# Second layer's scan inputs: deltas from nine stacked bf16 partial products in one matmul, the sum in one pass on DVE, the product with u on POOL

## The chip, the cores and the metric

The kernel runs on one core of a Trainium2 chip. Its engines work at the same time, each on its own queue of instructions: PE (TensorE, matrix products), DVE (VectorE) and POOL (GpSimd) for element-wise passes, ACT (ScalarE) for functions and copies, and SP, which here only issues transfers. They wait for one another through semaphores. The metric is the time of one execution on the device, in microseconds (us).

## What is computed

The program is a chain of four layers over 32 images of 96 channels and 32 x 32 points. The change lies in layer 1, a selective scan over 1024 points in both directions. Its reference, cut to what matters:

```python
flat = xc.reshape(b, d, L)
flipped = xc[:, :, ::-1, ::-1].reshape(b, d, L)
xl = jnp.swapaxes(jnp.concatenate([flat, flat, flipped, flipped], axis=1), 1, 2)
x_dbl = xl @ W_x
dt_r = x_dbl[..., :dr]
Bm = x_dbl[..., dr:dr + n]
Cm = x_dbl[..., dr + n:]
delta = jax.nn.softplus(dt_r @ W_delta + b_delta)
y = _selective_scan(xl, delta, A, Bm, Cm, Dp)
```

`dr` is 6 and `n` is 16. For each image the stage in question makes `delta` (768 channels by 1024 points), the product `delta * u` (u is `xl`), and `Bm` and `Cm`, all for the scans that follow.

## The kernel before

The program is a row of stages; each loads from and stores to the chip's main memory. The stage here is `l1_scan_inputs` (its tiles carry the prefix `l1p_`). It has its order written out by hand, one function per engine. `turns` runs a function `turn(k, s)` for each image k, unrolled by four, from one image ahead to one behind. Inside it loops over T = 6 steps, one per tile of 128 channels: tiles 0 to 2 in forward order, 3 to 5 backward. `back(k, t, lag)` names the tile that lies `lag` steps behind step t (it may belong to the image before), so each engine handles tiles of different age in one step. `nth(q)` is the semaphore value that says that item q is done.

For one image the work is:

- PE, `project` (L1255), in step 1 for the next image: `px` (38 rows: 16 of B, 16 of C, 6 of dt) from u, with the weights of equal halves added up in `wsum`; eight f32 matmuls of 512 columns.
- ACT, `read` (L1309), at the end of step 2: copies `px` to `dts`. A row of ones beneath it carries the bias.
- PE, `deltas` (L1262), in step t for tile t+2: two f32 matmuls of 512 columns over the 7 rows of dt and ones, into one of two halves of `pd`.
- DVE: `dl` = max(`pd`, 0) (L1225), `ab` = -2 `dl` + `pd`, that is -|x| (L1228), both in the tile's own step. ACT: exp (L1323) and ln(1 + .) (L1325) of it into `ln`. POOL: `dl` = `dl` + `ln` (L1206), which is softplus.
- DVE: `du` = `dl` * u (L1234), three steps behind (DU = 3). PE: `turn_du` (L1271), eight transposes of it into `pt`, four behind (TURN = 4), ahead of the step's deltas in PE's queue. ACT: copy of `pt` to `dut` (L1317), five behind (OUT = 5), ahead of the step's exp.
- PE, `turn_b` (L1277), in step 3: eight small matmuls that transpose the rows of B; ACT copies the result (L1331). SP stores `dls`, `duts`, `crows` and `bts`, and loads u for three images ahead.

Which wait holds what: `deltas` waits until `ab` of the tile two before is made; `turn_du` waits for `du` and for the copy of the transposes before, since `pt` is single.

```python
pe.wait_ge(dtc, nth(m))
pe.wait_ge(absd, nth(T * m + v - 2))
```

Of the kernel before, what the change touches and what calls it, by code (L numbers as in the profile page):

```python
# [20 lines left out]
F8 = mybir.dt.float8e5  # L21
ALU = mybir.AluOpType
# [1088 lines left out]
def l1_scan_inputs(nc, u1, w, dls, duts, bts, crows, ident):  # L1111
# [3 lines left out]
    DT = slice(2 * N, XD + 1)  # L1115
    U_OF = (0, 0, 1)
    DU, TURN, OUT = 3, 4, 5

    with ExitStack() as stack:
        r = Room(nc, "l1p", stack)  # L1120
        u = r.sb("u", [128, UNROLL, 2, HW])
        dts = r.sb("dts", [XD + 1, 2, HW])
# [5 lines left out]
        wx = r.sb("wx", [128, T, XD]); wsum = r.sb("wsum", [128, 4, XD]); wd = r.sb("wd", [XD + 1, T, 128])  # L1128
# [8 lines left out]
        const, wsummed, xd, dtc, btm, btc, dtm, plus, absd, expd, lnd, sumd, dud, dutm, dutc, passed = r.step_sems(  # L1137
            "const", "wsummed", "xd", "dtc", "btm", "btc", "dtm", "plus", "absd", "expd", "lnd", "sumd", "dud", "dutm",
            "dutc", "passed")
        consts = [(wx[:, :, :], w["wx"]), (wd[DT, :, :], w["wd"]), (idt[:, :], ident)]  # L1140
# [7 lines left out]
        def in_order(s, t):  # L1148
            row = u[:, s % UNROLL, U_OF[t % HT], :]
            return row[:, ::-1] if t >= HT else row  # L1150

        with nc.Block() as block:
            @block.sync
            def _(sp):
# [6 lines left out]
                def turn(k, s):  # L1161
                    for t in range(T):
                        m, v = back(k, t, 3)
# [4 lines left out]
                        m, v = back(k, t, 6)  # L1168
                        if v % HT == HT - 1 and there(m):
                            g = v // HT  # L1170
                            sp.wait_ge(dutc, nth(T * m + v))
# [3 lines left out]
                        if t == 3 and there(k + 1):  # L1175
                            p = (s + 1) % 2
                            sp.wait_ge(dtc, nth(k + 1))
                            sp.sem_inc(passed, 1)
                            sp.dma_start(one(crows, k + 1), dts[N:2 * N, p, :]).then_inc(s_c[p], 16)
                            sp.wait_ge(dud, nth(T * (k - 1) + T - 1))  # L1180
                            sp.sem_inc(passed, 1)
                            if there(k + 3):
                                load(k + 3, s + 3)
# [17 lines left out]
            def _(pool):  # L1201
                def turn(k, s):
                    if there(k):
                        for t in range(T):
                            pool.wait_ge(lnd, nth(T * k + t))
                            pool.tensor_tensor(dl[:, t, :], dl[:, t, :], ln[:, t % 3, :], ALU.add).then_inc(sumd, 1)  # L1206
# [4 lines left out]
            def _(dve):  # L1211
                dve.memset(dts[DT, :, :], 1.0).then_inc(const, 1)
# [1419 lines left out]
```

## Time and profile before

| | us |
|---|---|
| median of three runs | 22473.82 |
| lowest and highest | 22467.68, 22474.48 |
| profiled execution | 22468.44 |
| its span, first to last instruction | 22466.7 |

The profile of one execution lists for each engine when it was at work, and what it waited for when it was not. The granted clock is a share of TensorE's full 2.4 GHz; its two levels are 0.50 (1.2 GHz) and 1.00. Over the whole span PE is busy 19369.5 us (86%), DVE 17043.7 (76%), ACT 16452.2 (73%) and POOL 13494.5 (60%), at a mean granted clock of 0.913. These are means over stages that differ much: the stage of the change takes some 1220 us of the 22467, and what the change is worth is read there. In the trace an f32 matmul appears as two records; a group's mean ns is that of one record.

### The profile page before, as it was taken

What the parts mean: (1) busy time and instruction counts of PE and PEld (TensorE: products, weight loads), DVE (VectorE), ACT (ScalarE), POOL (GpSimd) and SP (SyncE); (2) the same over time, 40 slices, a digit from 0 to 9 for tenths busy, and PEclk for the clock granted to TensorE, in tenths of its full rate; (3) what the DMA queues carried; (4) which work ended last, traced back from release to release, by engine and by line L of the source; (5) the groups of instructions that cost most, each with busy time, mean ns of one, the idle gap of its engine ahead of it and who ended that gap; (6) DMA issues with size and microseconds to landing.
All of it is one profiled execution on the core that took longest, in us unless ns stands there. A gap on an engine that the chain in (4) does not pass through costs nothing. (4 is left out here: it accounts for less than half of the span.)

```text
span 22466.7 us, 264583 instructions
## 1 busy us (share of the span) xinstructions
PE 19369.5 (86%) x73736; PEld 10093.5 (45%) x73736; DVE 17043.7 (76%) x13056; ACT 16452.2 (73%) x25994; POOL 13494.5 (60%) x5860
## 2 busy tenths in 40 slices
PE   7788887788886889989998988889899888889798
PEld 2344443344442334434445555555555555235353
DVE  2777777777775659937669999999999998446666
ACT  6488886688882455556569999999999998124545
POOL 0277774377771558806349999999999998000101
PEclk8699998799996899998679999999999999569899
DMA  4566665566666341174543333333333333520202
GB/s 123 187 206 191 204 193 177 191 204 194 203 198 175 91 162 77 62 260 186 198 178 121 121 121 121 121 120 115 118 122 121 120 122 111 134 76 28 84 29 79
DMA packets 842186, 3171.46 MB, mean 141 GB/s; under 512 B 101515, under 2 KB 124541, under 8 KB 815750
## 3 DMA queue, kind: packets, MB, share of 16 engines
q1 hardware_dynamic: 805510, 3029.73, 41.2%
q10 hardware_dynamic: 35328, 125.85, 1.7%
q8 instruction: 591, 9.68, 0.2%
q14 instruction: 757, 6.20, 0.1%
HBM read 2316.32 MB, written 838.88 MB: 140 GB/s over the span
## 5 line engine op out<-in xcount | busy, mean ns | idle before, releaser
L1525 DVE TENSOR_TENSOR_SCAN l1s_h<-l1s_da,l1s_pd 128x1024 f32<-128x1024 f32 x3072 | 6862.7, 2275 | 389.5 <-PE l1s_pd L1460 378.6
L1556 ACT ACTIVATE l1s_dm<-l1s_dut,l1s_bt 128x384 f32<-128x384 f32 x8192 | 4449.7, 605 | 16.6 <-DMA l1s_u<-u 11.3
L1460 PE MATMUL l1s_pd<-l1s_id,l1s_dm 128*128 128x128 f32 x24576 | 3197.1, 277 | 609.9 <-ACT l1s_dm L1556 358.3
L1460 PEld LDWEIGHTS l1s_pd<-l1s_id,l1s_dm 128*128 128x128 f32 x24576 | 2756.3, 142 | 2033.7 <-DVE l1s_h L1525 1061.2
L1546 ACT ACTIVATE l1s_da<-l1s_dl,l1s_a 128x1024 f32<-128x1024 f32 x3072 | 3504.0, 1141 | 18.4 <-DVE l1s_h L1525 17.1
L1436 POOL TENSOR_TENSOR l1s_sm<-l1s_h 128x1024 f32<-128x1024 f32 x1024 | 2429.0, 2372 | 264.6 <-DVE l1s_h L1525 253.9
L1441 POOL TENSOR_TENSOR l1s_pb<-l1s_h,l1s_cc 128x1024 f32<-128x1024 f32 x1024 | 2433.4, 2376 | 1.1
L1445 POOL TENSOR_TENSOR l1s_pa<-l1s_sm,l1s_cc 128x1024 f32<-128x1024 f32 x1024 | 2428.8, 2372 | 0.0
L2318 POOL TENSOR_TENSOR l0sb_pr<-l0sb_h,l0sb_cc 128x1024 f32<-128x1024 f32 x768 | 1812.2, 2360 | 775.7 <-DVE l0sb_h L2391 718.0
L2318 POOL TENSOR_TENSOR l0sf_pr<-l0sf_h,l0sf_cc 128x1024 f32<-128x1024 f32 x768 | 1812.1, 2360 | 774.9 <-DVE l0sf_h L2391 713.6
L849 POOL TENSOR_TENSOR dw_acc<-dw_acc,dw_prod 128x961 f32<-128x961 f32 (+3 forms) x704 | 1572.8, 2275 | 1092.6 <-ACT dw_prod L802 1085.0
L1470 PE MATMUL l1s_py<-l1s_pb,l1s_id 128*128 128x512 f32 x4096 | 1991.4, 609 | 166.4 <-POOL l1s_pb L1441 162.6
L2081 POOL CAST ffn_h<-ffn_z 128x1024 fp8e5<-128x1024 f16 x128 | 181.6, 1420 | 3241.9 <-DVE ffn_z L2101 3221.4
L1470 PE MATMUL l1s_py<-l1s_pa,l1s_id 128*128 128x512 f32 x4096 | 1927.3, 593 | 0.0
L780 PE MATMUL dw_pc<-dw_vol,dw_diag 128*128 128x512 f32 (+7 forms) x4224 | 1763.7, 580 | 57.8 <-DMA dw_vol<-n 30.6
L2444 ACT ACTIVATE l0sb_dm<-l0sb_dut,l0sb_bt 128x192 f32<-128x192 f32 x4096 | 1491.8, 441 | 317.3 <-PE l0sb_pd L2328 307.9
L2444 ACT ACTIVATE l0sf_dm<-l0sf_dut,l0sf_bt 128x192 f32<-128x192 f32 x4096 | 1491.8, 440 | 316.2 <-PE l0sf_pd L2328 306.8
L879 DVE SCALAR_TENSOR_TENSOR dw_pc<-dw_vol,dw_wt,dw_pc 128x961 f32<-128x961 f32 (+5 forms) x1280 | 1484.7, 1235 | 209.2 <-PE dw_pc L780 205.2
L2347 PE MATMUL l0sb_py<-l0sb_pr,l0sb_id 128*128 128x512 f32 x3072 | 1579.0, 596 | 0.0
L2347 PE MATMUL l0sf_py<-l0sf_pr,l0sf_id 128*128 128x512 f32 x3072 | 1578.0, 596 | 0.0
L2385 DVE TENSOR_TENSOR_SCAN l0sb_h<-l0sb_da,l0sb_st,l0sb_pd 128x512 f32<-128x512 f32 x768 | 982.0, 1279 | 617.1 <-ACT l0sb_da L2434 568.4
L2385 DVE TENSOR_TENSOR_SCAN l0sf_h<-l0sf_da,l0sf_st,l0sf_pd 128x512 f32<-128x512 f32 x768 | 982.0, 1279 | 616.0 <-ACT l0sf_da L2434 567.8
(291 smaller groups left out, 31044.3 us busy)
## 6 DMA issues: line engine op xcount, KB each, us to landing
l1s_cc<-crows SPq DMA_DIRECT2D x1024, 512.0 KB, 3.7
l0sf_cc<-l0crowsf SPq DMA_DIRECT2D x512, 512.0 KB, 5.0
l0sb_cc<-l0crowsb SPq DMA_DIRECT2D x512, 512.0 KB, 5.0
l0sf_cc<-l0crowsf SPq DMA_DIRECT2D x512, 256.0 KB, 6.4
l0sb_cc<-l0crowsb SPq DMA_DIRECT2D x512, 256.0 KB, 6.3
dls<-l1p_dl SPq DMA_DIRECT2D x192, 512.0 KB, 6.9
duts<-l1p_dut SPq DMA_DIRECT2D x64, 1536.0 KB, 7.0
l1s_dut<-duts SPq DMA_DIRECT2D x64, 1536.0 KB, 7.2
```

The lines of the kernel that those rows point to most:

```text
L1436: pool.tensor_tensor(sm[:, rnd % 2, :], h[:, rnd * HT % 4, :], h[:, (rnd * HT + 1) % 4, :], ALU.add)\
L1441: pool.tensor_tensor(pb[:, rnd % 2, :], h[:, (rnd * HT + 2) % 4, :], cc[:, rnd % 4, :], ALU.mult)\
L1445: pool.tensor_tensor(pa[:, rnd % 2, :], sm[:, rnd % 2, :], cc[:, rnd % 4, :], ALU.mult)\
L1460: mm = pe.transpose(pd[:, s % 2, blk * 128:blk * 128 + 128], dm[:, rnd % 2, blk, j * 128:j * 128 + 128], idt[:, :])
L1470: mm = pe.matmul(target[:, hs], idt[:, :], prods[:, rnd % 2, hs], start=(n == 0), stop=(n == N - 1))
L1525: dve.tensor_tensor_scan(h[:, s % 4, :], da[:, j, :], pd[:, s % 2, :], 0.0, ALU.mult, ALU.add)\
L1546: act.activation(da[:, j, :], dl[:, half, j, :], ACT.Exp, scale=a[:, HT * half + j, n:n + 1])\
L1556: ins = act.activation(dm[:, rnd % 2, blk, :], dut[:, half, blk, :], ACT.Identity, scale=bt[:, half, blk, n:n + 1])
L2318: pool.tensor_tensor(pr[:, s % 4, :], h[:, s % 6, :], cc[:, rnd % 4, j, :], ALU.mult).then_inc(prod, 1)
L2347: mm = pe.matmul(py[:, j, HALVES[half]], idt[:, :], pr[:, s % 4, HALVES[half]], start=(n == 0), stop=(n == N - 1))
L2385: dve.tensor_tensor_scan(h[:, s % 6, LO], da[:, s % 4, LO], pd[:, 0, :], st[:, rnd // N, rnd % N, j:j + 1], ALU.mult, ALU.add).then_inc(sc ...
L2444: ins = act.activation(dm[:, rnd % 2, blk, cols], dut[:, rnd // N, blk, cols], ACT.Identity, scale=bt[:, rnd // N, q, blk, rnd % N:rnd % N ...
```

## The change

`dt` is held as three bf16 parts that add up to it: high, middle and low. The weights of the projection now have 128 columns, so `px` has 128 rows: 32 of B and C, and three groups of 32 that each hold dt three times (18 rows) and three rows of ones. The ones come from an added matmul with one row (`one_at`, `one_row`) in each half of the projection. Rows 32 to 127 of `parts` become, group by group, the high part (ACT's copy, which rounds), the middle part (DVE: `rest` = `px` - high; ACT: its copy) and the low part (DVE: `rest` - middle). `wd` is split into three bf16 parts likewise, once, by DVE at the start of the stage. Each group meets all three parts of the weights, so one bf16 matmul over 128 rows adds nine partial products and the bias. B and C go to a tile of their own, `bc`, through a second copy on ACT.

-|x| is made by setting the sign bit of `pd` on DVE; max and sum are one DVE pass, in the next step; POOL multiplies by u. The copy of `pt` goes to DVE for even tiles and stays on ACT for odd ones, in both cases four steps behind (OUT = 4), behind the step's other work. `read` moves ahead of step 2's exp, as two copies.

The diff, cut to its core:

```diff
-    DU, TURN, OUT = 3, 4, 5
+    TURN, OUT = 4, 4
+    GROUPS = slice(64, 128)
+
+    SIGN = -2 ** 31
...
             def _(pool):
...
-                            pool.wait_ge(lnd, nth(T * k + t))
-                            pool.tensor_tensor(dl[:, t, :], dl[:, t, :], ln[:, t % 3, :], ALU.add).then_inc(sumd, 1)
+                            q = T * k + t
+                            pool.wait_ge(sumd, nth(q))
+                            pool.wait_ge(dutm, nth(q - 2))
+                            pool.tensor_tensor(du[:, t % 2, :], dl[:, t, :], in_order(s, t), ALU.mult).then_inc(dud, 1)
...
             def _(dve):
...
                         if there(k):
                             q = T * k + t
-                            dve.wait_ge(s_dl[t], k * 16)
-                            dve.wait_ge(dud, nth(q - T))
                             dve.wait_ge(dtm, nth(q))
-                            dve.tensor_scalar(dl[:, t, :], pd[:, t % 2, :], 0.0, None, ALU.max).then_inc(plus, 1)
-                            dve.wait_ge(plus, nth(q))
                             dve.wait_ge(expd, nth(q - 3))
-                            dve.scalar_tensor_tensor(out=ab[:, t % 3, :], in0=dl[:, t, :], scalar=-2.0,
-                                                     in1=pd[:, t % 2, :], op0=ALU.mult, op1=ALU.add).then_inc(absd, 1)
-                        m, v = back(k, t, DU)
+                            dve.tensor_scalar(ab[:, t % 3, :].bitcast(I32), pd[:, t % 2, :].bitcast(I32), SIGN, None, ALU.bitwise_or).then_inc(absd, 1)
+                        m, v = back(k, t, 1)
                         if there(m):
-                            dve.wait_ge(sumd, nth(T * m + v))
-                            dve.wait_ge(dutm, nth(T * m + v - 2))
-                            dve.tensor_tensor(du[:, v % 2, :], dl[:, v, :], in_order(s + (t - DU) // T, v), ALU.mult)\
-                               .then_inc(dud, 1)
+                            q = T * m + v
+                            dve.wait_ge(s_dl[v], m * 16)
+                            dve.wait_ge(dud, nth(q - T))
+                            dve.wait_ge(lnd, nth(q))
+                            dve.scalar_tensor_tensor(out=dl[:, v, :], in0=pd[:, v % 2, :], scalar=0.0, in1=ln[:, v % 3, :],
+                                                     op0=ALU.max, op1=ALU.add).then_inc(sumd, 1)
+                        m, v = back(k, t, OUT)
+                        if v % 2 == 0 and there(m):
+                            dve.wait_ge(dutm, nth(T * m + v))
+                            dve.wait_ge(s_du[v // HT], m * 16)
+                            dve.tensor_copy(*place(s, v)).then_inc(evened, 1)
+                        if t == 2 and there(k + 1):
+                            dve.wait_ge(hi, nth(k + 1))
+                            dve.wait_ge(mid, nth(k))
+                            dve.tensor_tensor(rest[GROUPS, :], px[GROUPS, :], parts[GROUPS, p, :], ALU.subtract).then_inc(res, 1)
+                        if t == 3 and there(k + 1):
+                            dve.wait_ge(mid, nth(k + 1))
+                            dve.tensor_tensor(parts[96:128, p, :], rest[96:128, :], parts[96:128, p, :], ALU.subtract)\
+                               .then_inc(lo, 1)
...
             def _(pe):
...
-                                mm = pe.matmul(px[0:XD, hs], wsum[:, c, :], row[:, hs], start=(c == 0), stop=(c == 3))
+                                pe.matmul(px[:, hs], wsum[:, c, :], row[:, hs], start=(c == 0), stop=False)
+                            mm = pe.matmul(px[:, hs], one_at[:, :], one_row[:, hs], start=False, stop=True)
...
-                        pe.wait_ge(dtc, nth(m))
-                        pe.wait_ge(absd, nth(T * m + v - 2))
+                        pe.wait_ge(lo, nth(m))
+                        pe.wait_ge(sumd, nth(T * m + v - 2))
                         for hs in HALVES:
-                            mm = pe.matmul(pd[:, v % 2, hs], wd[DT, v, :], dts[DT, (s + (t + 2) // T) % 2, hs],
+                            mm = pe.matmul(pd[:, v % 2, hs], wdel[:, v, :], parts[:, (s + (t + 2) // T) % 2, hs],
                                            start=True, stop=True)
...
             def _(act):
...
+                        if t == 2 and there(k + 1):
+                            act.wait_ge(xd, nth(k + 1))
+                            act.wait_ge(dtm, nth(T * (k - 1) + T - 1))
+                            act.activation(parts[:, p, :], px[:, :], ACT.Copy).then_inc(hi, 1)
+                            act.wait_ge(btm, nth(k - 1))
+                            act.wait_ge(s_c[p], (k + 1 - p) * 8)
+                            act.activation(bc[:, p, :], px[0:2 * N, :], ACT.Copy).then_inc(bcd, 1)
                         if there(k):
...
                         if t == 2 and there(k + 1):
-                            read()
+                            act.wait_ge(res, nth(k + 1))
+                            act.activation(parts[GROUPS, p, :], rest[GROUPS, :], ACT.Copy).then_inc(mid, 1)
+                        m, v = back(k, t, OUT)
+                        if v % 2 and there(m):
+                            act.wait_ge(dutm, nth(T * m + v))
+                            act.wait_ge(s_du[v // HT], m * 16)
+                            act.activation(*place(s, v), ACT.Copy).then_inc(odded, 1)
```

How the rows stand on two engines, in the middle of the stage. DVE before, a step and the first two passes of the next:

```order
L1225 TENSOR_SCALAR l1p_dl<-l1p_pd 128x1024
L1228 SCALAR_TENSOR_TENSOR l1p_ab<-l1p_dl,l1p_pd 128x1024
L1234 TENSOR_TENSOR l1p_du<-l1p_dl,l1p_u 128x1024
L1225 TENSOR_SCALAR l1p_dl<-l1p_pd 128x1024
L1228 SCALAR_TENSOR_TENSOR l1p_ab<-l1p_dl,l1p_pd 128x1024
```

Each step is the same three passes, max, -|x| and the product with u; none reads `pt`. DVE in the change, from step 1 to step 4 of an image (L1258 is abs, L1265 the sum of the tile before, L1271 the copy of transposes, L1275 `rest`, L1278 `lo`):

```order
L1258 TENSOR_SCALAR l1p_ab<-l1p_pd 128x1024
L1265 SCALAR_TENSOR_TENSOR l1p_dl<-l1p_pd,l1p_ln 128x1024
L1258 TENSOR_SCALAR l1p_ab<-l1p_pd 128x1024
L1265 SCALAR_TENSOR_TENSOR l1p_dl<-l1p_pd,l1p_ln 128x1024
L1271 COPY l1p_dut<-l1p_pt 128x8x128
L1275 TENSOR_TENSOR l1p_rest<-l1p_px,l1p_parts 64x1024
L1258 TENSOR_SCALAR l1p_ab<-l1p_pd 128x1024
L1265 SCALAR_TENSOR_TENSOR l1p_dl<-l1p_pd,l1p_ln 128x1024
L1278 TENSOR_TENSOR l1p_parts<-l1p_rest,l1p_parts 32x1024
L1258 TENSOR_SCALAR l1p_ab<-l1p_pd 128x1024
L1265 SCALAR_TENSOR_TENSOR l1p_dl<-l1p_pd,l1p_ln 128x1024
L1271 COPY l1p_dut<-l1p_pt 128x8x128
```

The product with u has gone, and in every second step a copy that reads PE's transposes stands between the sum and the next abs.

PE in the change around the projection, from step 1 to step 4 (L1316 is `turn_du`, L1307 `deltas`, L1299 and L1300 the projection, L1323 `turn_b`):

```order
L1316 MATMUL l1p_pt<-l1p_id,l1p_du 128x128 x8
L1307 MATMUL l1p_pd<-l1p_parts,l1p_wdel 128x512 x2
L1299 MATMUL l1p_px<-l1p_u,l1p_wsum 128x512 x4
L1300 MATMUL l1p_px<-l1p_one,l1p_oneat 128x512
L1299 MATMUL l1p_px<-l1p_u,l1p_wsum 128x512 x4
L1300 MATMUL l1p_px<-l1p_one,l1p_oneat 128x512
L1316 MATMUL l1p_pt<-l1p_id,l1p_du 128x128 x8
L1307 MATMUL l1p_pd<-l1p_parts,l1p_wdel 128x512 x2
L1316 MATMUL l1p_pt<-l1p_id,l1p_du 128x128 x8
L1307 MATMUL l1p_pd<-l1p_parts,l1p_wdel 128x512 x2
L1323 MATMUL l1p_px<-l1p_id,l1p_bc 128x16 x8
L1316 MATMUL l1p_pt<-l1p_id,l1p_du 128x128 x8
```

The order on PE is as before, but for the two added matmuls of the projection. What changed for it is which semaphore the deltas wait for.

## Rows read from the trace of the kernel before

**Rows 1.** Stretches: us, busy us of each engine (count), mean granted clock, DMA share, GB/s
```profile
10500.00:11500.00 1000.00, 998.66 (x2772) 466.29 (x2770) 604.57 (x477) 511.67 (x529) 372.85 (x159) 0.64 0.52 196
...
12500.00:13000.00 500.00, 449.38 (x2231) 277.56 (x2229) 475.31 (x218) 499.44 (x767) 487.32 (x210) 1.00 0.34 125
```

**Rows 2.** Groups by line, 10500 to 11500: engine, shapes, count, busy us, mean ns, idle before
```profile
L1262 PE MATMUL l1p_pd<-l1p_dts,l1p_wd 7*128 7x512 f32 x636 | 511.8, 946 | 0.2 <-DVE l1p_ab L1228 0.2
L1206 POOL TENSOR_TENSOR l1p_dl<-l1p_dl,l1p_ln 128x1024 f32<-128x1024 f32 x159 | 374.3, 2354 | 630.4 <-ACT l1p_ln L1325 630.4
L1271 PE MATMUL l1p_pt<-l1p_id,l1p_du 128*128 128x128 f32 x1272 | 263.2, 375 | 1.2 <-ACT l1p_dut L1317 1.1
...
L1228 DVE SCALAR_TENSOR_TENSOR l1p_ab<-l1p_dl,l1p_pd 128x1024 f32<-128x1024 f32 x159 | 194.1, 1221 | 11.8
L1323 ACT ACTIVATE l1p_ln<-l1p_ab 128x1024 f32<-128x1024 f32 x159 | 167.1, 1051 | 34.7 <-DVE l1p_ab L1228 25.4 <-POOL l1p_dl L1206 9.2
...
L1317 ACT ACTIVATE l1p_dut<-l1p_pt 128x1024 f32<-128x1024 f32 x159 | 161.9, 1018 | 183.3 <-PE l1p_pt L1271 182.8
```

**Rows 3.** Waits, 10500 to 11500: who for whom, total us, times, longest
```profile
ACT l1p_dts L1309 <- PE l1p_px L1255: 266.2, 27, 10.7
DVE l1p_du L1234 <- PE l1p_pt L1271: 208.5, 27, 8.6
```

**Rows 4.** Timeline, one step: start us, duration, engine, line, operation, shapes, idle before
```profile
10985.56 1.97 PE L1271 MATMUL l1p_pt<-l1p_id,l1p_du 128*128 128x128 f32 x8
10985.66 1.22 DVE L1225 TENSOR_SCALAR l1p_dl<-l1p_pd 128x1024 f32<-128x1024 f32 x1 [1.55 <-PE l1p_pd L1262]
10987.01 1.22 DVE L1228 SCALAR_TENSOR_TENSOR l1p_ab<-l1p_dl,l1p_pd 128x1024 f32<-128x1024 f32 x1
...
10987.45 3.78 PE L1262 MATMUL l1p_pd<-l1p_dts,l1p_wd 7*128 7x512 f32 x4
...
10991.16 1.97 PE L1271 MATMUL l1p_pt<-l1p_id,l1p_du 128*128 128x128 f32 x8
```

**Rows 5.** Timeline, the projection of an image and what follows it
```profile
10996.77 9.28 PE L1255 MATMUL l1p_px<-l1p_u,l1p_wsum 128*38 128x512 f32 x16
...
11005.98 1.10 PE L1271 MATMUL l1p_pt<-l1p_id,l1p_du 128*128 128x128 f32 x8
...
11007.00 1.98 PE L1262 MATMUL l1p_pd<-l1p_dts,l1p_wd 7*128 7x512 f32 x4
...
11007.18 1.22 DVE L1234 TENSOR_TENSOR l1p_du<-l1p_dl,l1p_u 128x1024 f32<-128x1024 f32 x1 [7.83 <-PE l1p_pt L1271]
```

**Rows 6.** Timeline, DVE's and POOL's passes one image apart
```profile
10972.58 2.36 POOL L1206 TENSOR_TENSOR l1p_dl<-l1p_dl,l1p_ln 128x1024 f32<-128x1024 f32 x1 [11.72 <-ACT l1p_ln L1325]
...
10973.75 2.27 DVE L1234 TENSOR_TENSOR l1p_du<-l1p_dl,l1p_u 128x1024 f32<-128x1024 f32 x1
...
11011.42 2.27 DVE L1234 TENSOR_TENSOR l1p_du<-l1p_dl,l1p_u 128x1024 f32<-128x1024 f32 x1
```

**Rows 7.** Stretches of 1.5 us: the clock column before and in a projection
```profile
10972.00:10973.50 1.50, 1.50 (x18) 1.33 (x16) 1.47 (x2) 1.41 (x2) 0.92 (x1) 1.00 0.78 235
...
10975.00:10976.50 1.50, 1.50 (x8) 1.17 (x7) 1.50 (x2) 1.25 (x3) 0.41 (x1) 0.50 0.92 336
...
11000.50:11002.00 1.50, 1.50 (x3) 0.31 (x2) 0.00 (x0) 0.00 (x0) 0.00 (x0) 0.74 0.00 0
```

**Rows 8.** Timeline, 512-column fp8 matmuls of the last stages, low level and high
```profile
20952.20 0.59 PE L2145 MATMUL ffn_ph<-ffn_x,ffn_w 96*128 96x512 fp8e5 x2
...
20958.29 1.91 PE L2145 MATMUL ffn_ph<-ffn_x,ffn_w 96*128 96x512 fp8e5 x4
```

**Rows 9.** Timeline, weight loads of 16-row matmuls, high level here and low in layer 0
```profile
10420.22 1.52 PEld L1277 LDWEIGHTS l1p_px<-l1p_id,l1p_dts 16*128 16x128 f32 x13 [2.14 <-ACT l1p_dts L1309]
...
1023.77 2.56 PEld L442 LDWEIGHTS l0pf_pt<-l0pf_id,l0pf_dts 16*128 16x128 f32 x13 [0.84 <-issue]
```

**Rows 10.** Timeline, the stage's first projection
```profile
10409.77 9.21 PE L1255 MATMUL l1p_px<-l1p_u,l1p_wsum 128*38 128x512 f32 x16 [22.43 <-DMA l1p_u<-u]
```

More of the change, by code:

```diff
@@ L1121, in l1_scan_inputs @@
         u = r.sb("u", [128, UNROLL, 2, HW])
-        dts = r.sb("dts", [XD + 1, 2, HW])
+        parts = r.sb("parts", [128, 2, HW], BF16); rest = r.sb("rest", [128, HW]); bc = r.sb("bc", [2 * N, 2, HW])
         ab, ln = (r.sb(n, [128, 3, HW]) for n in ("ab", "ln"))
@@ L1136, in l1_scan_inputs @@
         s_du = [r.dma_sem(f"du{g}") for g in range(2)]
[L1137 to L1140, printed above, removed]
+        const, wready, xd, hi, bcd, res, mid, lo, btm, btc, dtm, absd, expd, lnd, sumd, dud, dutm, evened, odded, passed = r.step_sems(
+            "const", "wready", "xd", "hi", "bcd", "res", "mid", "lo", "btm", "btc", "dtm", "absd", "expd", "lnd", "sumd", "dud",
+            "dutm", "evened", "odded", "passed")
+        consts = [(wx[:, :, :], w["wx"]), (wd[:, :, :], w["wd"]), (which[:, :], w["which"]), (idt[:, :], ident)]
         ready = 16 * len(consts)
@@ L1162, in turn @@
                     for t in range(T):
-                        m, v = back(k, t, 3)
+                        m, v = back(k, t, 2)
                         if there(m):
@@ L2502, in build @@
     dls1 = dram("dls1", (IMAGES, 6, 128, HW)); ys1 = dram("ys1", (IMAGES, 4, 128, HW))
-    ws = {n: w[f"{n}_1"] for n in ("wx", "wd", "alog", "skip", "ln_g", "ln_b", "wo")} | {"avg192": w["avg192"]}
+    ws = {n: w[f"{n}_1"] for n in ("wx", "wd", "which", "alog", "skip", "ln_g", "ln_b", "wo")} | {"avg192": w["avg192"]}
     l1_scan_inputs(nc, u1, ws, dls1, duts, bts, crows, w["ident"])
@@ L2588, in arranged @@
     w["l1dw_b"] = twice(v["L1_conv_b_dw"])
-    w["wx_1"] = tiles(bc_first(v["L1_conv_W_x"])[order], 6)
-    w["wd_1"] = cat([v["L1_conv_W_delta"], v["L1_conv_b_delta"][None]])[:, order].reshape(RANK + 1, 6, 128)
+    wx, wd = v["L1_conv_W_x"], np.zeros((128, 4 * DI), f)
+    thrice = [np.tile(wx[:, :RANK], 3), np.zeros((4 * DI, 32 - 3 * RANK), f)]
+    w["wx_1"] = tiles(cat([wx[:, RANK:], *thrice * 3], 1)[order], 6)
+    which = np.zeros((128, 3), f)
+    for j in range(3):
+        for group in range(3):
+            rows = slice(32 + 32 * group + RANK * j, 32 + 32 * group + RANK * (j + 1))
+            wd[rows], which[rows, j] = v["L1_conv_W_delta"], 1
+        wd[32 + 3 * RANK + j], which[32 + 3 * RANK + j, j] = v["L1_conv_b_delta"], 1
+    w["wd_1"], w["which_1"] = wd[:, order].reshape(128, 6, 128), which
     w["alog_1"] = tiles(v["L1_conv_A_log"][order], 6)
```

79 lines of the change are left out of this document (46 added, 33 removed).

## The prediction

> **What bounds it now.** The change touches one stage, `l1_scan_inputs`, whose trace runs from 10404 to about 11625 us. I read it in four steps.
>
> First the stretch view [rows 1]. In 1000 us of this stage PE is busy 998.66 us, DVE 604.57, ACT 511.67 and POOL 372.85, at a mean granted clock of 0.64. PE is the bound, and it runs mostly at the lower of its two levels. The scan stage at 12500 us stands beside it at 1.00.
>
> Second, the period of one image. Two like passes of `du` start at 10973.75 and 11011.42 us [rows 6], so an image takes 37.67 us; 32 of them are 1205 us, the whole stage but its ends.
>
> Third, what fills a period. In an ordinary step at the low level, the eight transposes start at 10985.56, the delta matmuls (four records for two f32 matmuls) at 10987.45 and take 3.78 us, and the next transposes start at 10991.16 [rows 4]: 5.60 us a step, all of it PE. DVE's passes take 1.22 us each and ACT's 1.05 or 1.02 [rows 2]; they wait for PE and have room. Once per image comes the projection, 9.28 us [rows 5].
>
> Fourth, who waits across that projection. DVE's `du` waits 7.83 us for the transposes behind it [rows 5], 208.5 us in total, and ACT's copy of its result 266.2 us [rows 3]. So while PE projects, the others already stand still; only PE's own work is saved by a faster matmul.
>
> The clock: 0.50 at 10975, while PE is never idle, 0.74 in the 1.5 us from 11000.50, some 4.5 us into the projection, and 1.00 at 10972, behind the projection of the image before [rows 7].
>
> **PE's saving.** Deltas go from f32 with 7 rows to one low-precision pass with 128 rows. The nearest rows are the fp8 matmuls of 512 columns: four in 1.91 us at the low level, two in 0.59 at the high one [rows 8]. With 0.63 us for the last one, the four are 0.43 apart, so two take 1.06 us to be ready, and occupy PE for 0.86, instead of 3.78 and 3.7. That is 2.85 us a step, 17 us an image if all steps were cold. Two things go back. The two added one-row matmuls cost 0.43 or 0.21 us each, 0.5 together. And `turn_b` now reads partitions 0 to 15 beside deltas that fill all rows; before it ran interleaved with the 7-row deltas. Alone, 13 of its weight loads take 1.52 us at the high level and 2.56 at the low one [rows 9], so its 16 cost 2.0 or 3.2 us. If PE remained the bound, an image would need at the low level 6 x (1.97 + 0.86) + 3.2 + 9.8 = 30 us. It won't, and that is the core of this prediction.
>
> **The new chain.** Before, deltas(t+2) waited for `absd`(t), made in DVE's step t. Now they wait for `sumd`(t), and DVE makes that one step later, after abs(t+1); and abs(t+1) needs deltas(t+1). So PE and DVE take turns: deltas, abs, sum, deltas. Second, DVE now copies the transposes of even tiles, in its queue directly behind the sum. Those transposes stand in PE's queue behind the deltas that this very sum releases. DVE therefore waits for deltas plus transposes, copies, and only then does the next abs, which holds the exp, ln, sum and deltas behind it. I take 0.1 us for a hand-over to PE, 1.2 for each DVE pass (1.22 in [rows 2, 4]; the copy, the 64-row and the 32-row pass have no row of their own and are taken by their 1024 columns), and walk one image from the start of its projection, at the clock levels that the rows show there:
>
> (a) projection 9.3 + 0.5 = 9.8. (b) Transposes of tile 4 of the image before, which stand behind it: 1.0 (1.10 less overlap, [rows 5]). ACT's copy to `parts` and `bc`, then exp and ln of tile 2, run beside (b) and (c) and end 4.1 us after the projection, in time. (c) DVE: copy, `rest`, abs(3), sum(2): 4.8. (d) deltas(4) 0.1 + 1.06 = 1.2, beside DVE's `lo` pass of 1.2, then abs and sum 2.4: 3.6. (e) deltas(5) 0.96, `turn_b` 3.2, transposes 1.97, then copy, abs, sum 3.6: 9.7. (f) a step without a DVE copy: 1.2 + 2.4 = 3.6. (g) a step with one: 0.96 + 1.97 + 1.2 + 2.4 = 6.5. (h) as (f), 3.6. (i) deltas(3), in front of the next projection: 1.0.
>
> Sum 43.6 us against 37.67: +5.93 an image, +190 us for 32. In it are 9.0 us, at (e) and (g), in which DVE only waits for PE's deltas, `turn_b` and transposes; before, DVE's passes ran beside such work.
>
> **The rest.** POOL does the multiply by u instead of an add, 2.35 us a tile [rows 2]; half are read backwards, for which POOL has no row, but it is idle 63% of the stage and the transposes come three steps later, so even a doubled time is covered. ACT gives away three of six copies (3 x 1.02) and gets one more 1024-column copy of `px` and one of `rest`: about 19 us of 43.6, covered. On SP the stores of `dls` and `duts` move one step forward, behind waits that are by then met; a tile is stored a whole image before it is rewritten; nobody waits. The load of u three images ahead has slack. Once per run come seven weight passes of 768 columns, by 1.22 us for 1024 some 0.95 us each, four small ones and 128-column weights to load. The first projection waited for u anyway until 10409.77 [rows 10], which hides part; I take 5 us, bounds 0 and 10.
>
> Total: 190 + 5 = +195 us. The profiled execution took 22468.44 us, 1.7 outside its span, and lies 0.02% below the median 22473.82. On the median: 22669 us, 0.87% slower.
>
> **Rivals.** *The clock stays high* (B). The walk takes the low level from some microseconds behind the projection on. For the high level speaks the scan stage, where transposes and f32 matmuls of full height share PE at 1.00 [rows 1]; the new deltas are of full height too. Against it: PE would be at work for 20 of the 34 us between projections, 12 of them transposes, and it sat at 0.50 even while never idle [rows 4, 7]. All high, the terms become 7.5, 1.0, 4.8, 3.6, 7.2, 3.1, 5.2, 3.1 and 0.5, together 36.0 us: 1.67 less than now, or -53 + 5 = -48 us, 22426. Partly high ends between, up to 22600. Beside this stands the Trainium skill, TensorE: Matmul & The Clock Gate, Part 4: a transpose does not count as PE being busy for the clock. By that rule PE would look nearly idle between projections, and B would fall away for A's 22669; by the scan stage alone, B's 22426 would be the likelier. No row here shows a stretch of transposes alone.
>
> *DVE's 32-row pass collides with POOL* (C). It reads two SBUF tensors, and it is queued just where sum(2) releases POOL's multiply. The row for that: POOL works from 10972.58 to 10974.94, a DVE pass over two SBUF tensors started at 10973.75 and took 2.27 instead of 1.22, ending 1.08 after POOL [rows 6]. If POOL gets in first, `lo` ends 2.36 + 1.08 + 0.1 = 3.5 us after the sum instead of 1.2: +2.1 an image beyond the deltas, +67 us, 22736. It needs no semaphore that is late, so I expect DVE to be first. The Trainium skill says the same of the mechanism (GPSIMD Engine Reference, Specifications: the SBUF interfaces are shared, with contention for DVE instructions with two SBUF inputs), and the trace agrees with its 2.27 us.
>
> *The chain is hidden* (D). If the queues slip against each other so that DVE's passes run beside PE's work as now, the stage falls to the busiest engine: DVE 12 x 1.2 + 3 x 1.2 + 2.4 = 20.4 us, plus the projection, in which DVE waits, and hand-overs: about 31 us. (31 - 37.67) x 32 + 5 = -208 us, 22266. For it: all busy sums fall well under the period. Against: the waits in the order of the queues leave no slip; the copy of tile t-4 cannot start before sum(t-1) is done.
>
> *The matmul does not get shorter* would leave +190 as a lower bound, and I give it nothing apart.
>
> **How the numbers follow.** Forecast A, a period of 41.5 to 46 us, 22602 to 22746: 0.60. B 0.13: 0.05 faster, 0.06 within 0.2%, 0.02 slower. C 0.12. D 0.10. Something dearer still, such as a projection that rises to the high level later: 0.05. A, C, the parts of B that are not faster and half of the dear end make 0.83: 22450 to 22790. About 0.2%, 45 us, is what a measurement can tell from no change. Faster by more: 0.15 (D and B's part); within: 0.06; slower: 0.79. In the period's terms, slower needs more than 38.9 us.
>
> **What would show it.** In the changed trace: the delta matmuls near 1.1 us for two at the low level; PE busy about 70% of the stage, with idle time ended by DVE's sum; DVE's copy with about 3 us of idle ahead of it, 6 where `turn_b` stands in front, 10 across the projection; the clock near 0.6; a period near 43.6. A period under 38 at a clock of 0.9 is B; `lo` at over 2 us is C; a copy that waits for nothing is D, and the walk is wrong.

## The result, and the profile after

| | us |
|---|---|
| changed kernel, median of four runs | 22685.79 |
| lowest and highest | 22676.91, 22688.67 |
| kernel before, on the same chip, median of four | 22470.75 |
| ratio, with 95% interval | 1.0096 (1.0078 to 1.0113) |

It is 215 us slower, 0.96%; the forecast was 195 us slower, 22669 us. The span of the profiled execution grew from 22466.7 to 22684.9, by 218. From the first transfer of `l1_scan_inputs` to the first of the next stage it took 1234.0 us before (10402.90 to 11636.93) and takes 1451.8 now (10402.53 to 11854.28), 218 more as well. The scan stage at 12500 us has its 450 us of PE in 500 as before. So all of the loss lies in the stage that was changed.

The stretch view of the changed kernel (columns as in [rows 1]):

```profile
10500.00:11500.00 1000.00, 647.64 (x2090) 401.76 (x2124) 458.94 (x386) 421.71 (x430) 319.78 (x136) 0.61 0.43 169
12500.00:13000.00 500.00, 450.15 (x2223) 279.84 (x2222) 472.81 (x217) 497.59 (x764) 484.67 (x210) 0.99 0.33 116
```

Set against [rows 1]: PE has fallen from 998.66 to 647.64 us of 1000, at nearly the same clock, DVE from 604.57 to 458.94, ACT and POOL too. Every engine is less busy, and POOL's 136 passes in place of 159 say how much less gets done. No engine is near its bound any more; a chain of waits has taken its place.

The groups by line and the waits, 10500 to 11500, answer [rows 2] and [rows 3]:

```profile
L1316 PE MATMUL l1p_pt<-l1p_id,l1p_du 128*128 128x128 f32 x1088 | 243.5, 399 | 0.0
...
L1307 PE MATMUL l1p_pd<-l1p_parts,l1p_wdel 128*128 128x512 bf16 x238 | 126.7, 621 | 353.5 <-DVE l1p_dl L1265 353.5
...
L1271 DVE COPY l1p_dut<-l1p_pt 128x1024 f32<-128x1024 f32 x68 | 83.3, 1225 | 482.1 <-PE l1p_pt L1316 482.1
```

```profile
DVE l1p_dut L1271 <- PE l1p_pt L1316: 482.1, 68, 12.1
PE l1p_pd L1307 <- DVE l1p_dl L1265: 353.5, 136, 5.6
...
ACT l1p_parts L1352 <- PE l1p_px L1300: 236.8, 22, 10.8
```

The delta matmuls were 511.8 us of PE and are 126.7. Ahead of them PE idles 353.5 us, and all of it is ended by DVE's sum (L1265). DVE in turn stands 482.1 us ahead of its copy, for PE's transposes. PE and DVE take turns, as the forecast said. ACT's wait for the projection is no loss: it stood 266.2 us there before [rows 3].

One image on PE, from one projection to the next (start, duration; in brackets the idle time before and who ended it; of the pair of deltas at 11002.74 the first record is missing):

```profile
10972.26 5.89 PE L1299 MATMUL l1p_px<-l1p_u,l1p_wsum 128*128 128x512 f32 x8
10978.09 0.39 PE L1300 MATMUL l1p_px<-l1p_one,l1p_oneat 1*128 1x512 bf16 x1
10978.41 3.70 PE L1299 MATMUL l1p_px<-l1p_u,l1p_wsum 128*128 128x512 f32 x8
10982.04 0.38 PE L1300 MATMUL l1p_px<-l1p_one,l1p_oneat 1*128 1x512 bf16 x1
10982.36 1.09 PE L1316 MATMUL l1p_pt<-l1p_id,l1p_du 128*128 128x128 f32 x8
10988.54 1.03 PE L1307 MATMUL l1p_pd<-l1p_parts,l1p_wdel 128*128 128x512 bf16 x2 [5.09 <-DVE l1p_dl L1265]
10989.36 1.91 PE L1316 MATMUL l1p_pt<-l1p_id,l1p_du 128*128 128x128 f32 x8
10992.30 1.04 PE L1307 MATMUL l1p_pd<-l1p_parts,l1p_wdel 128*128 128x512 bf16 x2 [1.02 <-DVE l1p_dl L1265]
10993.27 3.59 PE L1323 MATMUL l1p_px<-l1p_id,l1p_bc 16*128 16x16 f32 x16
10996.79 1.97 PE L1316 MATMUL l1p_pt<-l1p_id,l1p_du 128*128 128x128 f32 x8
11002.74 0.63 PE L1307 MATMUL l1p_pd<-l1p_parts,l1p_wdel 128*128 128x512 bf16 x1 [3.98 <-DVE l1p_dl L1265]
...
11016.63 5.90 PE L1299 MATMUL l1p_px<-l1p_u,l1p_wsum 128*128 128x512 f32 x8
```

The same on DVE:

```profile
10983.49 1.22 DVE L1271 COPY l1p_dut<-l1p_pt 128x1024 f32<-128x1024 f32 x1 [12.11 <-PE l1p_pt L1316]
...
10988.51 1.22 DVE L1278 TENSOR_TENSOR l1p_parts<-l1p_rest,l1p_parts 32x1024 bf16<-32x1024 f32 x1
...
10998.80 1.22 DVE L1271 COPY l1p_dut<-l1p_pt 128x1024 f32<-128x1024 f32 x1 [6.55 <-PE l1p_pt L1316]
...
11003.50 1.22 DVE L1258 TENSOR_SCALAR l1p_ab<-l1p_pd 128x1024 int32<-128x1024 int32 x1 [1.22 <-PE l1p_pd L1307]
...
11008.69 1.23 DVE L1271 COPY l1p_dut<-l1p_pt 128x1024 f32<-128x1024 f32 x1 [2.84 <-PE l1p_pt L1316]
...
11027.86 1.22 DVE L1271 COPY l1p_dut<-l1p_pt 128x1024 f32<-128x1024 f32 x1 [12.11 <-PE l1p_pt L1316]
```

From copy to copy it is 44.37 us, where [rows 6] gave 37.67; by the count of tiles (136 / 6 images in 1000 us) the mean is 44.1. The copy waits 2.84, 6.55 and 12.11 us at the three places that the forecast named with 3, 6 and 10. Where no copy stands in between, it is abs that waits for the deltas, 1.22 us at 11003.50.

### The profile page after: what moved, and what is told of

It reads as the page before. It is cut to its first block and busy times, and to the rows that moved or that the text cites. A ratio compares the mean times of both kernels' runs of the same rounds, so it can differ in the third digit from the quotient of the medians.

```text
span 22684.9 us, 264136 instructions
## 1 busy us (share of the span) xinstructions
PE 19086.2 (84%) x73368; PEld 10096.3 (45%) x73416; DVE 16964.6 (75%) x13033; ACT 16430.4 (72%) x25962; POOL 13495.5 (59%) x5860
```

## The experiments

The change has two parts that can be had singly: the matmul (deltas from stacked bf16 parts, instead of f32 over 7 rows) and the order (which pass of DVE, ACT and POOL stands where, and what the deltas wait for). The forecast says that the order costs and the matmul saves. The first five runs below test the chain of waits. `deltas_twice` was meant to test it too, against two other accounts; its time did not follow the chain at a fixed clock, and the runs after it test the clock.

### The matmul alone: `only_stacked_deltas`

The kernel before, its order kept (max, -|x| and the product with u on DVE; copies on ACT five steps behind; deltas wait for `absd`), with `parts`, `rest`, `bc`, `wdel` and the bf16 matmul of the change:

```diff
-                            mm = pe.matmul(pd[:, v % 2, hs], wd[DT, v, :], dts[DT, (s + (t + 2) // T) % 2, hs],
+                            mm = pe.matmul(pd[:, v % 2, hs], wdel[:, v, :], parts[:, (s + (t + 2) // T) % 2, hs],
```

> The kernel before with the stacked bf16 deltas alone: projection to 128 rows, parts, rest, lo, bc and the one bf16 matmul per half, all as in the change; but the order of before for the rest: max and -|x| in two DVE passes in the tile's own step, the add on POOL, the product with u on DVE three steps behind, all copies of transposes on ACT five behind, deltas waiting for -|x|. rest stands in DVE's step 3 and lo in step 4. Chain theory: deltas no longer wait for the sum, PE runs two tiles ahead and its 17 us saving per image is kept: about 31.5 to 33 us an image, the program about 22280 to 22330 us, the fastest so far. Added-work theory: it carries all the added work (rest, lo, two copies, one-row matmuls, turn_b alone), so it would lose against the kernel before, above 22500. Clock theory: PE is as little busy as in the changed kernel or less, so its level stays low; if that were the loss it would show here too.

Measured: 22259.43 us, ratio 0.9908 (0.9891 to 0.9925). The matmul alone wins 211 us. The stretch view:

```profile
10500.00:11300.00 800.00, 621.21 (x2447) 365.00 (x2447) 699.17 (x523) 555.61 (x575) 375.09 (x157) 0.78 0.65 244
```

PE is busy 78% and DVE 87%: now DVE is close to the bound, with the three passes that it had before, `rest` and `lo`. The time lies 21 us below the range that was expected of the chain. The clock went to 0.78, though PE was busy less than before; the clock theory of the expectation had it stay low. So 22685.79 - 22259.43 = 426 us is what the order costs on top of this matmul.

### The order alone: `f32_deltas_new_order`

The changed kernel with `dts`, `wd` and the f32 matmuls over 7 rows of before (`rest` and `lo` fall away):

```diff
-                            mm = pe.matmul(pd[:, v % 2, hs], wdel[:, v, :], parts[:, (s + (t + 2) // T) % 2, hs],
+                            mm = pe.matmul(pd[:, v % 2, hs], wd[DT, v, :], dts[DT, (s + (t + 2) // T) % 2, hs],
```

> The kernel before with the new order alone: deltas stay two f32 matmuls over 7 rows, projection and dts as before (no parts, rest, lo, bc, no one-row matmuls), but -|x| by the sign bit, the sum on DVE one step later, the product with u on POOL, DVE copying even tiles and ACT odd ones four steps behind, ACT's read of the projection ahead of step 2's exp, deltas waiting for the sum. It is the fourth corner of a square: kernel before (f32, old order) 22471, only_stacked_deltas (bf16, old order) 22259, changed kernel (bf16, new order) 22686. Chain theory: the new order puts each 3.8 us of deltas on the chain; by the walk an image takes 55 us, the program about 23030 us. Additive theory (the order costs 22686 - 22259 = 427 us whatever the matmul is): about 22900 us. Added-work theory: the order adds no work, so about 22471.

Measured: 22994.7 us, ratio 1.0232 (1.0215 to 1.0249), 524 us slower than before. That lies between the 22900 of a fixed price for the order and the 23030 of the chain, nearer to the chain. DVE's timeline:

```profile
10974.66 1.23 DVE L1238 TENSOR_SCALAR l1p_ab<-l1p_pd 128x1024 int32<-128x1024 int32 x1 [3.96 <-PE l1p_pd L1278]
10975.80 1.21 DVE L1245 SCALAR_TENSOR_TENSOR l1p_dl<-l1p_pd,l1p_ln 128x1024 f32<-128x1024 f32 x1
10990.51 1.23 DVE L1251 COPY l1p_dut<-l1p_pt 128x1024 f32<-128x1024 f32 x1 [13.50 <-PE l1p_pt L1287]
```

DVE's pass on `pd` now waits 3.96 us: the whole of the deltas stands on the chain, as it should if PE and DVE take turns. In the order of before the f32 deltas overlap DVE's passes: its pass on `pd` waits 1.55 us [rows 4].

### The copies one step later: `copies_step_later`

```diff
-    TURN, OUT = 4, 4
+    TURN, OUT = 4, 5
```

> The changed kernel with OUT = 5 instead of 4: both copies of the transposes, DVE's and ACT's, stand one step later in their queues; nothing else differs. Chain theory: DVE's copy then reads transposes that PE made a step before, so the 2 to 3 us wait in front of it in every second step goes, and the one across the projection too; what stays is turn_b in front of the transposes of tile 0. By the same walk as in the prediction an image takes about 39.3 us instead of 44.3, the program about 22530 us (165 less than the changed kernel, 57 more than the kernel before). Clock theory (the loss comes from PE standing at its low level): the work and the level stay, so the time stays within 20 us of the changed kernel's 22686. Added-work theory (two ACT copies, rest, lo, the added one-row matmuls and turn_b alone are the loss): also no change, 22686.

Measured: 22530.54 us, ratio 1.0029 (1.0017 to 1.0041), what was expected almost to the microsecond, and 155 us less than the changed kernel. That it costs to have the copies where the change puts them is thereby shown (this run moves DVE's and ACT's together). But the size came out by luck, as PE's timeline shows:

```profile
10998.85 3.70 PE L1299 MATMUL l1p_px<-l1p_u,l1p_wsum 128*128 128x512 f32 x8
11002.49 0.38 PE L1300 MATMUL l1p_px<-l1p_one,l1p_oneat 1*128 1x512 bf16 x1
11009.13 1.94 PE L1316 MATMUL l1p_pt<-l1p_id,l1p_du 128*128 128x128 f32 x8 [6.26 <-ACT l1p_dut L1370]
```

A new wait has come: `pt` is single, and its copy for the odd tile 3, on ACT, has slipped behind ACT's two copies of `px`, exp and ln. PE waits 6.26 us for it once per image. On DVE `lo` takes 2.22 us beside POOL's multiply, where it took 1.22 in the changed kernel:

```profile
10972.67 2.22 DVE L1278 TENSOR_TENSOR l1p_parts<-l1p_rest,l1p_parts 32x1024 bf16<-32x1024 f32 x1
```

Against these two losses the clock rose, from 0.61 to 0.77 over the stage. The walk had neither the losses nor the rise.

### The same with `turn_b` early: `copies_later_turnb_early`

`OUT` = 5, and `turn_b` in step 2, between transposes and deltas, where PE waits anyway:

```diff
                             turn_du(m, v)
+                        if t == 2 and there(k + 1):
+                            turn_b()
                         m, v = back(k, t, -2)
...
-                        if t == 3 and there(k + 1):
-                            turn_b()
```

> As copies_step_later, and turn_b moved on PE from the end of step 3 to step 2, between the transposes of tile 4 and the deltas of tile 4, where PE waits about 5 us for DVE's sum behind the projection. Chain theory: its 3.6 us leave the chain, an image takes about 35.8 us, the program about 22416 us, faster than the kernel before (22471). Clock theory and added-work theory: PE's work is the same, no difference from copies_step_later.

Measured: 22493.46 us (ten runs), ratio 1.0009 (0.9999 to 1.0018): 77 us slower than expected. The expectation rested on the walk of the run before, which had no wait of PE for ACT's copy. The waits view shows that wait here too:

```profile
PE l1p_pt L1316 <- ACT l1p_dut L1370: 230.3, 78, 6.3
```

### The wait taken away: `copies_split_turnb_early`

DVE's copies five steps behind, ACT's four as in the change, `turn_b` early as above:

```diff
-    TURN, OUT = 4, 4
+    TURN, OUT, ODD = 4, 5, 4
...
-                        m, v = back(k, t, OUT)
+                        m, v = back(k, t, ODD)
                         if v % 2 and there(m):
```

> As copies_later_turnb_early, but only DVE's copies of the even tiles stand one step later (OUT = 5); ACT's copies of the odd tiles stay where the change has them (four steps behind). In copies_later_turnb_early PE waited 6.26 us behind each projection for ACT's copy of tile 3, which had moved behind ACT's reading of the projection; the run before it missed its 35.8 us an image for that reason. Chain theory: this wait goes, an image takes 34 to 36 us, the program 22360 to 22430 us, around 22391. If something else held it back: no gain over 22493.

Measured: 22357.81 us, ratio 0.9947 (0.993 to 0.9963), 2 us below the expected range. With DVE's copy out of the chain, ACT's copy left where it was and `turn_b` in PE's idle time, this order takes 328 us less than that of the change, though the deltas wait for the same sum. In its waits view the line PE <- ACT is gone and PE's wait for the sum is down from 353.5 us to 206.6, none longer than 2.3:

```profile
PE l1p_pd L1307 <- DVE l1p_dl L1265: 206.6, 178, 2.3
```

No run moves DVE's copy alone, so how the 328 us divide between it and `turn_b` is open. So are the 98 us that this run still takes more than `only_stacked_deltas`: the wait for the sum that is left is one candidate, but no run gives the deltas back their earlier release within this order.

### More work on PE: `deltas_twice` and `only_stacked_twice`

Each pair of delta matmuls is issued twice, with the same result, in the changed kernel and in `only_stacked_deltas`:

```diff
-                        for hs in HALVES:
+                        for hs in HALVES * 2:
```

> The changed kernel with each pair of delta matmuls issued twice, into the same place: 0.86 us more of PE at the low level per step, the result is the same. Chain theory: every one of the six pairs of an image lies on the chain, so +5.1 us an image, +165 us, about 22850. Idle theory (PE is busy 65% of this stage and has room): no change, 22686. Clock theory: full-height matmuls double their share; if that lifts PE's level between the projections, the time rises by much less than 165 us or falls, and the mean granted clock of the stage goes well above 0.61.

> only_stacked_deltas with each pair of delta matmuls issued twice, into the same place, the result is the same. In that kernel the stage's clock was 0.76 and PE waited for ACT's copies. Clock theory: the clock rises, transposes and turn_b get shorter and pay for the added matmuls: 22230 to 22260 us, the same or up to 0.1% faster than only_stacked_deltas. If the clock does not rise: 6 x 0.86 us of PE more an image, partly in its idle time, up to 22330 us.

Measured: `deltas_twice` 22688.5 us, ratio 1.0099 (1.0082 to 1.0116), the same as the changed kernel, where the chain at a fixed clock gave +165 us and the clock theory much less. `only_stacked_twice` took 22234.27 us, ratio 0.9894 (0.9878 to 0.9911): with 12 more matmuls an image it is no slower than `only_stacked_deltas`; the intervals of the two ratios overlap. The stretch views, first of `deltas_twice`, then of `only_stacked_twice`:

```profile
10500.00:11500.00 1000.00, 662.74 (x2378) 388.51 (x2379) 456.22 (x383) 420.59 (x429) 316.11 (x135) 0.71 0.43 169
```

```profile
10500.00:11300.00 800.00, 637.12 (x2797) 367.19 (x2850) 720.24 (x537) 572.40 (x592) 387.47 (x162) 0.90 0.67 250
```

The clock went from 0.61 to 0.71 and from 0.78 to 0.90. PE's timeline of `deltas_twice` shows where the added work was paid back:

```profile
10975.21 1.88 PE L1307 MATMUL l1p_pd<-l1p_parts,l1p_wdel 128*128 128x512 bf16 x4 [3.58 <-DVE l1p_dl L1265]
...
10979.63 1.04 PE L1307 MATMUL l1p_pd<-l1p_parts,l1p_wdel 128*128 128x512 bf16 x4 [0.83 <-DVE l1p_dl L1265]
10980.50 3.60 PE L1299 MATMUL l1p_px<-l1p_u,l1p_wsum 128*128 128x512 f32 x8
```

Four matmuls take 1.88 us at the low level, 0.85 more than two; but the first half of the projection takes 3.60 us, not 5.89, since the high level is there before it starts. In some images more was paid back: `turn_b` took 1.96 us at 10956.21 and 3.59 at 11000.76. From projection to projection it is 44.5 us on average (10533.58 to 11468.67, 21 images) and from 43.1 to 47.3 in single ones. So here added matmuls of full height raised the granted clock, while the kernel before stood at 0.64 with PE almost never idle [rows 1]. What differs is that its deltas used 7 rows of the array; the next runs test that.

### The rows of the f32 deltas: `f32_deltas_128_rows` and `f32_deltas_64_rows`

The kernel before, with the same f32 matmuls in the same order, over 128 or 64 rows instead of 7. The added rows hold B, C or ones, and their weights are zero. `turn_b` can no longer run beside the deltas in either. With 128 rows (with 64 the slice ends at 64, and the tiles and weights grow to match):

```diff
-    DT = slice(2 * N, XD + 1)
+    DT = slice(0, 128)
```

> The kernel before with its f32 delta matmuls over 128 rows instead of 7: dts and wd have 128 rows, the weights of all but the seven rows are zero, so the sums are the same; everything else as before. It asks what holds PE's clock at the low level between projections in the kernel before, where PE is never idle. Height theory (matmuls over few rows do not lift the clock; doubled full-height matmuls in deltas_twice lifted the stage's mean from 0.61 to 0.71): the clock goes to 0.9 or more, PE's work per image falls to about 27 us, DVE becomes the bound at 28 to 31 us, the program 22170 to 22270 us. Transpose theory (transposes alone hold it low, rows do not matter): the clock stays at 0.64, and turn_b no longer runs beside the deltas, 2 to 3 us more an image: 22540 to 22570 us.

> As f32_deltas_128_rows (22147.6 us, stage clock 0.99), but over 64 rows instead of 128: half the array's height. turn_b reads rows 0 to 15 and so still cannot run beside the deltas, exactly as with 128 rows. If the loss of that overlap, or anything but the height, lifted the clock, this run is at 22148 +- 25 us with a clock of 0.99. If the height decides, and by degrees, the clock lies between 0.64 and 0.99 and the time between 22200 and 22500 us (22471 before, plus up to 1.6 us an image for turn_b alone at the low level = 22520). My guess is the middle, 22330.

Measured: 128 rows 22147.6 us, ratio 0.9855 (0.9839 to 0.9872), the fastest of all and 22 us below the range that was expected; 64 rows 22488.87 us (ten runs), ratio 1.0008 (0.9998 to 1.0017), no change. Stretch view and two groups with 128 rows, then the stretch with 64:

```profile
10500.00:11300.00 800.00, 735.49 (x3028) 374.85 (x3027) 715.58 (x529) 569.08 (x587) 418.38 (x177) 0.99 0.72 273
```

```profile
L1234 DVE TENSOR_TENSOR l1p_du<-l1p_dl,l1p_u 128x1024 f32<-128x1024 f32 x178 | 312.1, 1754 | 59.3 <-PE l1p_pt L1271 59.3
...
L1271 PE MATMUL l1p_pt<-l1p_id,l1p_du 128*128 128x128 f32 x1417 | 190.8, 278 | 56.4 <-ACT l1p_dut L1317 56.4
```

```profile
10500.00:11300.00 800.00, 800.00 (x2179) 363.13 (x2177) 471.68 (x377) 404.81 (x418) 294.74 (x126) 0.68 0.52 194
```

With 64 rows PE is never idle and sits at 0.68, as before at 0.64 [rows 1]; with 128 rows it is at 0.99. The matmuls, their columns and their order are alike, so what decides here is the rows of the array that the deltas use. The loss of the overlap with `turn_b` is in both and doesn't do it. The 64-row result, 22489 us, lies at the dear end of its range, far from the 22330 that was guessed: 64 rows lifted the clock hardly at all, and no height between 64 and 128 was run.

### Both: `f32_deltas_128_new_order`

`f32_deltas_new_order` with the deltas over 128 rows.

> The order of the change with f32 deltas over 128 rows (the weights of all rows but the 7 real ones are zero, the rows themselves hold B, C or ones); nothing else differs from f32_deltas_new_order (22994.7 us, stage clock 0.59), and the matmul instructions, their columns and their order are the same. Height theory (matmuls over 7 of 128 rows leave the clock low, full-height ones lift it): the stage rises to 0.9 or more, and the walk at the high level with two f32 matmuls at 1.96 us gives projection 7.2, transposes 1.0, DVE 3.6, then 4.5, 8.5, 4.5, 6.6, 4.5 and 2.0, together 42.4 us an image instead of the 53.9 that f32_deltas_new_order would need by its time: 22995 - 32 x 11.5 = 22627 us, 22590 to 22720 with a partly low stage. Rival (the rows don't matter, the clock of f32_deltas_128_rows rose only because turn_b no longer ran beside the deltas, or by its denser queue): here PE waits in turns anyway, so the clock stays near 0.6 and the time at 22995 us, with turn_b behind the deltas up to 23060.

Measured: 22763.97 us, ratio 1.013 (1.0114 to 1.0147). The clock rose from 0.59 to 0.82 and the time fell by 231 us, on a kernel whose PE waits in turns. The height of the deltas works here too. The time was 137 us above the 22627 of the walk and 44 above the range. The level doesn't hold through the whole image:

```profile
10977.34 1.95 PE L1293 MATMUL l1p_px<-l1p_id,l1p_dts 16*128 16x16 f32 x16
10979.23 1.09 PE L1287 MATMUL l1p_pt<-l1p_id,l1p_du 128*128 128x128 f32 x8
10983.90 3.78 PE L1278 MATMUL l1p_pd<-l1p_dts,l1p_wd 128*128 128x512 f32 x4 [3.58 <-DVE l1p_dl L1245]
...
10990.22 1.98 PE L1278 MATMUL l1p_pd<-l1p_dts,l1p_wd 128*128 128x512 f32 x4 [0.83 <-DVE l1p_dl L1245]
```

After `turn_b`, one set of transposes and 3.58 us of waiting, the deltas run at the low level, in 3.78 us; the pair after them is back at the high one, in 1.98.

The times side by side, in us:

| deltas | order of before | order of the change |
|---|---|---|
| f32, 7 rows | 22471 | 22995 |
| f32, 64 rows | 22489 | not run |
| f32, 128 rows | 22148 | 22764 |
| bf16 parts, 128 rows | 22259 | 22686 |

In each line that has both, the order costs: 524, 616 and 426 us. The price depends on the matmul that it is paid with; it isn't a fixed sum.

## Why the prediction was right, point by point

**What bounded it.** Right as far as it went: PE was never idle and the others waited. But "only PE's own work is saved by a faster matmul" left out that PE's work at 0.64 was long because of the clock, and the clock low because of the 7 rows. The fastest kernel here saves no PE instruction at all. PE was busy 65% of the changed stage, where the forecast named about 70%.

**The chain.** Right, and shown by three runs that touch it: `f32_deltas_new_order` put the longer deltas on it (DVE waits 3.96 us for them), `copies_step_later` and `copies_split_turnb_early` took the copy out of it. The copy's wait across the projection, 12.11 us, was named with 10; the walk's own terms (i), (a) and (b) add up to 11.8, so that was a slip in naming the wait and not in the sum.

**The terms.** From the two timelines of the changed kernel, measured against forecast: (a) projection 10.2 against 9.8; (b) 1.1 against 1.0; (c) 5.0 against 4.8; (d) 3.8 against 3.6; (e) 10.0 against 9.7, taking the deltas at 11002.74 to start 0.4 us earlier for the missing record; (f) 3.6 against 3.6; (g) 6.3 against 6.5; (h) 3.6 against 3.6; (i) 0.8 against 1.0. Together 44.4 us against 43.6. The two that were mis-sized most: the projection, 0.4 us over the 9.28 of [rows 5] plus 0.5 for the one-row matmuls, and `turn_b`, which took 3.59 us where the row scaled to 16 gave 3.2. By the mean of 44.1 the loss is 32 x (44.1 - 37.67) = 206 us. The walk held the clock at the levels of the rows of before, and the sum came out because the change stood at much the same level, 0.61 against 0.64; the experiments show that it can't be relied on.

**The deltas.** Two took 1.03 us at the low level; the estimate from fp8 rows [rows 8] was 1.06.

**The start.** First deltas at 10421.58 us before and at 10431.90 after: 10.3 us, where 5 was taken, with an upper bound of 10. The projection starts 4.9 us later, at 10414.63, since it waits for DVE's passes over the weights, though these took less than was assumed (0.41 to 1.04 us each). It takes 1.6 us longer. From its end to the first deltas 6.4 us pass instead of 2.6: `rest`, ACT's copy of it and a `turn_b` of 3.56 us (1.4 before) stand in front of them, which the term left out. 206 + 10 makes 216, beside the 215 measured.

**POOL, ACT, SP.** Hidden, as forecast. POOL's product with reversed reads took 2.35 us like the others, so the doubled time that was allowed for did not come.

**Rival B, the clock stays high.** It did not in the change: 0.61. The evidence named for B, that the new deltas are of full height, was the right thought. The evidence against it, "it sat at 0.50 even while never idle", was read wrongly: that low level was one of 7-row matmuls, and says nothing of matmuls over 128 rows. What kept B away was how little such work there is between the waits: one more pair of matmuls a step brought 0.71, and f32 pairs of full height in the same order brought 0.82. So A's time came out right with the clock held fixed, but B was set aside by a wrong argument, and where the work changed, a fixed clock failed: the +165 us that it gave for `deltas_twice` came out at nothing.

Of the rule that was weighed there, `f32_deltas_128_rows` is the run that bears on it. It spends 190.8 of 735.5 us of PE in transposes, 26%, the same share as before (263.2 of 998.66, [rows 1, 2]), and stands at 0.99. Transposes at this share are thus compatible with the high level, and by themselves don't explain why the kernel before stood low. The Trainium skill (TensorE: Matmul & The Clock Gate, Part 4) says that the full clock doesn't engage for transposes, which don't count as PE being busy in the same way. These runs don't contradict it, as other matmuls ran in every stretch above. Transposes alone stand only at the end of the stage, as in `f32_deltas_128_rows` behind its last deltas at 11285.50:

```profile
11288.59 1.06 PE L1271 MATMUL l1p_pt<-l1p_id,l1p_du 128*128 128x128 f32 x8 [1.13 <-ACT l1p_dut L1317]
11292.12 1.94 PE L1271 MATMUL l1p_pt<-l1p_id,l1p_du 128*128 128x128 f32 x8 [2.46 <-ACT l1p_dut L1317]
```

The level falls from 1.00 to 0.50 between these two sets and stays there for the four that follow. That fits the Trainium skill, but PE also waits 1.1 to 2.6 us ahead of each set, so it doesn't tell transposes from waits.

Part 1 of the same page of the Trainium skill describes a clock that follows how busy PE has been. By the trace that is not enough, if busy is taken as the profile shows it: with 7 rows PE was at work 998.66 us of 1000 at 0.64 [rows 1], and with 128 rows 735.49 of 800 at 0.99.

**Rival C.** In the changed kernel `lo` took 1.22 us: no collision, as expected, but not because DVE came first. The prediction had sum(2) release POOL's multiply. All 136 multiplies in the 1000 us waited for PE's transposes instead, since `du` has two buffers (681.4 us in total); around `lo`, at 10988.51, POOL was idle from 10985.88 to 10991.36. The mechanism is real: in `copies_step_later`, where the queues stand otherwise, `lo` took 2.22 us beside a multiply that started 1.21 us before it, and ended 1.08 us after that, as in [rows 6]. C's price was summed a little short: 3.5 less 1.2 is 2.3 us an image and not 2.1, so 22743 us.

**Rival D, the chain is hidden.** In the change no; but with the order of before around the new matmul it is what happened: 22259 us, where D gave 22266. That the two are so close is luck. D's sum for DVE was right for the change: 20.4 us an image against 20.2 measured (458.94 us in 22.7 images). `only_stacked_deltas` has other passes on DVE, busy 26.7 us an image (699.17 us, 523 passes of 20 an image), and DVE waits only 3.3 of the 9.8 us that D added for the projection (85.8 us, 26 times).

## What to carry to other kernels

When an engine gets faster, ask first who waits for whom in the new order: here the order took away 426 us and the faster matmul gave 211. Part of that was a copy put directly behind the pass that releases another engine's next work, so that the two engines took turns instead of working side by side. Let such a copy lag one step more, but check both engines that share the single buffer. And before saving work on PE in a stage whose granted clock is low while PE is never idle, look at how many rows its matmuls use: zero weights over the unused rows up to 128 are an edit of a few lines and gave 1.45%; up to 64 they gave nothing.

## What the runs showed of the hardware that I had not expected

- In this stage the granted clock went with the rows of the array that the deltas use, and not only with whether PE was at work. Same instructions, same order: 0.64 with 7 rows, 0.68 with 64 and 0.99 with 128. At a given level the rows didn't change the time: an f32 pair took 3.78 us at the low level with 7 rows [rows 4] and with 128, and 1.98 at the high level with 7 [rows 5] and with 128.
- More full-height work on PE cost nothing here: with the deltas issued twice the changed kernel took 22688.5 against 22685.8 us. The projection fell from 10.2 to 7.8 us in the image shown, and in some images `turn_b` from 3.59 to 1.96.
- `turn_b`, eight small matmuls in 16 records, ran interleaved with the 7-row deltas: before, the two together took 2.2 us at the high level (11009.93 to 11012.13), where a pair of deltas alone takes 1.98. Behind deltas that use its rows it takes 3.59 us at the low level, and 1.95 at the high one in `f32_deltas_128_new_order`. The Trainium skill (TensorE: Matmul & The Clock Gate, Part 3) describes small matmuls that run at the same time on different row groups of the array, and weight loads that overlap matmuls only where the row groups differ; the trace agrees with these numbers.
- The next bound of the fastest kernel is DVE, 715.58 us of 800, of which 0.53 us a tile is the slowing of `du`, which takes 1754 ns on average where it took 1.22 us with POOL idle [rows 5]. By the two passes of before that took 2.27 us [rows 6], both beside a pass of POOL, that is its collision with POOL; no run took POOL's pass away from it.
